# A four-layer graph network on one core: LayerNorm statistics two tiles at a time, a diagonal product moved to VectorE, two bias products moved to GpSimd, and a new order of the work

## The reference

```
L0: e = x@a_i [i] + x@a_j [j], normalised by its mean and variance over all pairs,
    e = e*adj + adj, leaky, softmax over i, h = sigmoid(alpha @ x)
L1: h = x@Wp + bp; masked GAT attention; h_gat = relu(layernorm(attn*A @ h))
    h_gin = (1+eps)*h_gat + A @ h_gat; z = relu(layernorm(h_gin@W1 + b1))
    out = relu(z@W2 + b2 + h_gat)
L2: A = softmax of the edge weights; out = diag(A) part @ (x@W0)
    + off-diagonal part @ (x@W1) + bias
L3: h = x@W; masked attention; elu(attn @ h)
```

## Time and profile before

| | before |
|---|---|
| median of three executions | 1191.42 us |
| span of the profiled execution, first to last instruction | 1188.6 us |
| PE / DVE / ACT / POOL busy | 93% / 89% / 81% / 50% |
| busy in 300 to 500 us of the span: PE / DVE / ACT / POOL | 195.76 / 189.68 / 175.35 / 110.70 of 200 us |
| granted TensorE clock in the loop | 1.00 (0.80 in the first 50 us) |

### The profile page before, as it was taken

How to read it: one execution, slowest core, us unless ns; L and a number is a source line. 1 busy time by engine, 2 the same in 40 slices (tenths; PEclk the granted TensorE clock), 3 DMA queues, 4 the chain that set the end, 5 groups by cost and what they waited for, 6 DMA issues and landing times.

```text
span 1188.6 us, 28920 instructions
## 1 busy us (share of the span) xinstructions
PE 1103.5 (93%) x7752; PEld 907.9 (76%) x7752; DVE 1055.8 (89%) x3894; ACT 964.7 (81%) x2453; POOL 594.6 (50%) x1250
## 2 busy tenths in 40 slices
PE   4779999999999999999999999999999999999964
PEld 3457777888777888887778888877778888788743
DVE  6887999999999999999999999999999899997642
ACT  3566888888888888888888889888888898888753
POOL 4243435555564555556555555555545554553422
PEclk7799999999999999999999999999999999999976
DMA  3010001110011111000111110101111010010000
GB/s 76 19 36 19 27 28 46 31 31 22 22 35 35 35 35 35 26 28 17 35 35 35 35 35 26 35 9 35 35 35 35 29 37 30 17 46 10 28 9 19
DMA packets 59478, 36.17 MB, mean 30 GB/s; under 512 B 3872, under 2 KB 54816, under 8 KB 59424
## 3 DMA queue, kind: packets, MB, share of 16 engines
q1 hardware_dynamic: 59424, 35.54, 10.0%
HBM read 18.75 MB, written 8.39 MB: 23 GB/s over the span
## 4 chain that ended last, share of the span: by engine, by line
PE 58%; POOL 10%; issue 9%; DVE 5%; ACT 2%; DMA 1%; POOLq 0%; SPq 0%; ACTq 0%; DVEq 0%
PE ps L965 14%; PE ps L893 7%; PE ps L949 6%; PE ps L982 4%; PE ps L1025 4%; PE ps L934 4%; PE ps L744 4%; PE ps L737 3%; POOL rirA L559 2%; PE ps L1014 2%; PE ps L880 2%; PE ps L1043 2%; PE ps L1042 2%; PE ps L919 1%; DMA xA<-in_x_dram 1%
## 5 line engine op out<-in xcount | busy, mean ns | idle before, releaser
L965 PE MATMUL ps<-hE,pTE 128*128 128x128 f32 x1024 | 131.0, 277 | 0.2
L982 PE MATMUL ps<-gin_j,hgat 128*128 128x512 f32 x256 | 124.4, 610 | 3.0 <-DVE gin_j L1495 1.8
L965 PE MATMUL ps<-hB,pTB 128*128 128x128 f32 x1024 | 125.3, 275 | 0.7 <-DVE pTB L1626 0.6
L893 PE MATMUL ps<-xsA,pA 128*128 128x128 f32 x1024 | 124.4, 275 | 0.0
L965 PEld LDWEIGHTS ps<-hE,pTE 128*128 128x128 f32 x1024 | 122.8, 193 | 0.9 <-issue 0.6
L1025 PE MATMUL ps<-att_j,xD 128*128 128x512 f32 x256 | 122.3, 601 | 0.8 <-ACT xD L2207 0.8
L965 PEld LDWEIGHTS ps<-hB,pTB 128*128 128x128 f32 x1024 | 119.4, 192 | 1.4 <-DVE pTB L1626 1.1
L893 PEld LDWEIGHTS ps<-xsA,pA 128*128 128x128 f32 x1024 | 119.4, 192 | 0.4 <-issue 0.3
L2250 ACT ACTIVATE pA<-vA,nmA,rirA 128x512 f32<-128x512 f32 x128 | 107.0, 845 | 6.3 <-DVE vA L1683 5.3
L2312 ACT ACTIVATE pE<-wE,mnE 128x512 f32<-128x512 f32 x128 | 92.4, 723 | 20.9 <-DVE mnE L1613 20.8
L1595 DVE SCALAR_TENSOR_TENSOR wE<-ps,hE,y2E 128x512 f32<-128x512 f32 x128 | 92.1, 739 | 13.8 <-ACT y2E L2282 13.7
(11 more groups left out here) (238 smaller groups left out, 3084.6 us busy)
## 6 DMA issues: line engine op xcount, KB each, us to landing
xA<-in_x_dram SPq DMA_DIRECT2D x32, 256.0 KB, 2.9
xrA<-in_x_dram SPq DMA_DIRECT2D x32, 256.0 KB, 2.7
xrB<-xB SPq DMA_DIRECT2D x32, 256.0 KB, 2.3
out_dram<-xout SPq DMA_DIRECT2D x32, 256.0 KB, 2.3
adj_i<-in_adj_dram SPq DMA_DIRECT2D x1, 1024.0 KB, 5.5
a<-in_L_gnn_a_dram SPq DMA_DIRECT2D x2, 64.0 KB, 5.1
w_sb<-in_L_gnn_W_dram SPq DMA_DIRECT2D x2, 64.0 KB, 3.7
l2w<-in_L_gnn_W_dram SPq DMA_DIRECT2D x2, 64.0 KB, 3.2
```

The lines of the kernel that those rows point to most:

```text
L893: last = mm(at("aggA")[:, i * P:(i + 1) * P], pA[:, j, i * P:(i + 1) * P], xsA[:, j], start=(j == 0), stop=(j == NT - 1))
L965: last = mm(at("agg" + n)[:, i * P:(i + 1) * P], att[n]["pT"][:, i, j], att[n]["h"][:, j, 0:P], start=(j == 0), stop=(j == NT - 1))
L982: last = mm(at("gin"), hgat[:, j], gin_j[:, j], start=(j == 0), stop=(j == NT - 1))
```

## The change

- **LayerNorm statistics.** bn_stats gets two tiles in one instruction, read as interleaved: element 0 of the first tile, element 0 of the second, element 1 of the first, and so on, 256 elements, with 512 bytes between neighbours in the order of reading. The instruction keeps statistics of even and odd elements apart, so its six results are the count, mean and squared deviation of either tile. Twelve bn_stats per graph take the place of 24, all 24 bn_aggr go, and `L["mean"]` and `L["m2"]` point into the results. rstd_k takes m2/128 + eps with one tensor_scalar on POOL, after the negative mean instead of ahead of it; for B it is a small DVE instruction, ve_B.
- **Diagonal part.** In the preparation the diagonal is spread over all partitions (spread_dia, copy_dia, a (128 x 512) tile diaT). Per graph, PE transposes xD (four transposes instead of four float32 products), and DVE multiplies the PSUM result with diaT into xTdD (diag_D). ACT's copy_xTD goes.
- **Two biases.** The bias products in x2_C and out_D go from PE. POOL adds b2 to hgat (bias_C, result hgb) and the layer-2 bias to xD (bias_D, result xDb), each one tensor_tensor of 128 x 512 with the bias row repeated; q_C and y_D read these. The split of the biases in the preparation covers 258 columns instead of 514.
- **Orders and banks.** All lists for PE, DVE, ACT and POOL are new, fill and drain included, and so is IN_BANK. SP's turn is as it was. The loop still has 22 turns.

```diff
+        def two_tiles(src, half):
+            return src[:, half * 2 * P:(half + 1) * 2 * P].rearrange("p (u d) -> p d u", u=2)
...
-                    pool.tensor_tensor(L["ve"][:], L["mv"][:, :, 1], eps, ALU.add).then_inc(s["ve_" + k], 1)
-                    pool.wait_ge(s["ve_" + k], g.now)
                     pool.wait_ge(s["applied0_B" if k == "B" else "applied_" + k], g.last)
-                    pool.tensor_tensor(L["nm"][:], L["mv"][:, :, 0], consts[:, 3:4].to_broadcast([P, NT]),
+                    pool.tensor_tensor(L["nm"][:], L["mean"], consts[:, 3:4].to_broadcast([P, NT]),
                                        ALU.mult).then_inc(s["nm_" + k], 1)
+                    if k != "B":
+                        pool.tensor_scalar(L["ve"][:], L["m2"], 1.0 / P, LN_EPS, ALU.mult, ALU.add).then_inc(s["ve_" + k], 1)
+                        pool.wait_ge(s["ve_" + k], g.now)
...
+            def bias_C(g):
+                pool.wait_ge(s["applied_B"], g.now)
+                pool.wait_ge(s["qC_ready"], g.last)
+                pool.tensor_tensor(hgb[:], hgat[:], bias_2, ALU.add).then_inc(s["hgb_ready"], 1)
+            def bias_D(g):
+                pool.wait_ge(s["applied_C"], g.now)
+                pool.wait_ge(s["y_D"], g.last)
+                pool.tensor_tensor(xDb[:], xD[:], bias_l2, ALU.add).then_inc(s["xDb_ready"], 1)
...
-                features("x2", zT, w2_sb[:], bias_2).then_inc(s["x2C_in_psum"], 1)
+                features("x2", zT, w2_sb[:]).then_inc(s["x2C_in_psum"], 1)
...
-                    last = mm(at("xTD")[:, i * P:(i + 1) * P], xD[:, i], dia[:, i], start=True, stop=True)
-                last.then_inc(s["xD_scaled"], 1)
+                transpose("xTD", xD).then_inc(s["xD_transposed"], 1)
...
-                mm(tiles(at("outD")), onesb[:], bias_l2, start=True, stop=False, skip_group_check=True)
...
-                    for i in range(NT):
-                        last = v.bn_stats(L["st"][:, i], y(i))
+                    for half in range(NT // 2):
+                        last = v.bn_stats(ln[k]["st"][:, half], two_tiles(src, half))
...
-                    for i in range(NT):
-                        last = v.bn_aggr(L["mv"][:, i], L["st"][:, i])
-                    last.then_inc(s["stats_" + k], 1)
...
+            def ve_B(g):
+                v.scalar_tensor_tensor(L["ve"][:], L["m2"], 1.0 / P, zzB[:], ALU.mult, ALU.add).then_inc(s["ve_B"], 1)
...
+            def diag_D(g):
+                dve.wait_ge(s["xD_transposed"], g.now)
+                dve.wait_ge(s["outD_ready"], g.last)
+                v.tensor_tensor(xTdD[:], at("xTD"), diaT, ALU.mult).then_inc(s["xTdD_ready"], 1)
...
-            def copy_xTD(g):
-                a.copy(xTdD[:], at("xTD")).then_inc(s["xTdD_ready"], 1)
...
-            [("tE", 5), ("z", 3)],
+            [("pB2", 3), ("h012E", 5), ("pE0", 5)],
```

More of the change, by code:

```diff
@@ new lines, in fill @@
+                t.once(triangles, numbers)
+                t.graph(0, variance_A, power_A, shift_A, high_A, rest_A0, middle_A)
+                t.once(loops_E)
+                t.graph(0, rest_A1, low_A)
+                t.graph(1, centre_A, square_A)
+                t.graph(0, rstd_A)
+                t.graph(1, variance_A, power_A, shift_A, high_A, rest_A0, middle_A, rest_A1, low_A)
+                t.graph(0, rstd_B)
+                t.graph(2, centre_A, square_A, variance_A, power_A, shift_A)
@@ L580, in fill @@
                 t.graph(1, rstd_A)
-                t.graph(0, rstd_Z)
-                t.once(loops_E, no_edge_E)
-                t.graph(0, rstd_C)
+                t.graph(2, high_A, rest_A0, middle_A, rest_A1, low_A)
+                t.graph(0, bias_C, rstd_Z, rstd_C)
                 t.graph(1, rstd_B)
-                t.graph(3, centre_A, square_A, variance_A, power_A, shift_A, high_A, rest_A0,
-                        middle_A, rest_A1, low_A)
+                t.graph(3, centre_A, square_A)
@@ L587, in fill @@
+                t.graph(0, bias_D)
+                t.graph(3, variance_A, power_A, shift_A)
                 t.graph(2, rstd_A)
+                t.graph(3, high_A, rest_A0, middle_A, rest_A1, low_A)
                 t.graph(1, rstd_Z)
+                t.once(no_edge_E)
+                t.graph(1, bias_C)
                 t.graph(0, rstd_D)
                 t.graph(1, rstd_C)
+                t.graph(4, centre_A, square_A)
                 t.graph(2, rstd_B)
-                t.graph(4, centre_A, square_A, variance_A, power_A, shift_A, high_A, rest_A0,
-                        middle_A, rest_A1, low_A)
+                t.graph(4, variance_A, power_A, shift_A)
@@ L594, in fill @@
                 t.graph(3, rstd_A)
-                t.graph(2, rstd_Z)
+                t.graph(4, high_A, rest_A0, middle_A, rest_A1, low_A)
+                t.graph(1, bias_D)
+                t.graph(2, bias_C, rstd_Z)
                 t.graph(1, rstd_D)
@@ L1704, in bn_B @@
                 dve.wait_ge(s["nm_B"], g.last)
-                for i in range(NT):
-                    last = v.bn_stats(ln["B"]["st"][:, i], at("aggB")[:, i * P:(i + 1) * P])
+                for half in range(NT // 2):
+                    last = v.bn_stats(ln["B"]["st"][:, half], two_tiles(at("aggB"), half))
                 last.then_inc(s["bn_B"], 1)
@@ L1832, in fill @@
+                t.graph(0, bn_C)
+                t.graph(1, bn_B, ve_B)
+                t.graph(3, dots_A0, dots_A1, mean_A)
+                t.graph(2, y_A)
+                t.graph(3, sumsq_A)
+                t.graph(2, bn_A)
                 t.graph(1, gain_B, offset_B)
-                t.graph(2, y_A, bn_A, join_A)
-                t.graph(3, v_A0, v_A1, lrelu_A0, lrelu_A1)
+                t.graph(0, diag_D)
+                t.graph(3, v_A0, v_A1, v_A2, v_A3, max_A, lrelu_A0, offset_A, lrelu_A1, lrelu_A2)
```

1436 lines of the change are left out of this document (688 added, 748 removed), and 9 rows, old and new, of the table IN_BANK.

## The result

The changed kernel takes 1233.71 us (1231.67 to 1235.83, 4 runs) against 1191.79 beside it; the ratio is 1.036, 95% interval [1.034, 1.038]. The forecast was 1168. The profiled run took 1235.83.

The account below looks back on a forecast made before the run. It took PE, the DVE/DMA path and POOL's vector chain as balanced, PE's turn falling from 33.75 to 33.0 us. 27 turns give -20.3, the ends -3: 1165.3 span, plus 2.8, 1168 us; range 1150 to 1194.

Parts of the forecast that it names:

- ACT's path: In the loop, last read of xA 26.5 us behind sum_A, plus 4.62 and 1.86: next sum_A at 33.0, as PE.
- the sum: PE's loop turn: 33.75 - 0.89 + 0.29 - 0.15 = 33.0 us, multiplied by 27 turns.
- The ends: Fill and drain together: -3 us, between 0 and -8; the new fill order was left unpriced.
- PE's work: Per turn on PE: bias products gone, -0.44 us, transposes for scale_xD's float32 products, -0.45; together -0.89.
- POOL's chain: rstd_A joins POOL's vector chain: wait ahead of rows_A on PE grows 0.29 us per turn, bounds -0.3 to +0.9.
- DVE: DVE's loop path: about 32.6 us per turn, just below PE's 33.0, so not bounding, 0.4 to spare.
- rival 1: POOL's long bias sums hold DVE 0.3 to 0.6 us each, or x2_C waits: turn 33.5 to 33.8, about 1186; chance 0.2.
- Rival 2: DVE's interleaved bn_stats read runs at half rate, 0.6 us instead of 0.33: turn 34.9, about 1220 us; chance 0.15.
- Rival 3: POOL's chain runs free of DVE, stall ahead of rows_A goes: turn 32.3, about 1148 us; chance 0.08.

Follow-up runs that it names:

- e1: Changed kernel with the next graph's xA load ahead of keep_xB and store in SyncE's queue; 1182.33 us, ratio 0.991 to the kernel before.
- e4: e1 with both bias products back on PE, POOL's two 128 x 512 sums gone; 1172.87 us, ratio 0.983 to the kernel before.
- e14: Changed kernel with only the fill mended: POOL's masks ahead of the first centring, weights' transposes and copies late; 1227.96 us, ratio 1.028 to the kernel before.
- e15: e4 with the fill mended as in e14, and rstd_A moved behind low_A on POOL; 1192.26 us.
- e7: e1 with bias_D and rstd_Z exchanged in POOL's turn, both sums on POOL; 1184.11 us, ratio 0.993 to the kernel before.
- e2: Changed kernel with the xA load between keep_xB and store in SyncE's queue; 1199.53 us, ratio 1.005 to the kernel before.

## Why the prediction was wrong, point by point

**The step that failed is ACT's path**, "with 4.62 and 1.86 the next sum_A is at 33.0". The working up to it held: the last read of xA was foretold 26.5 behind sum_A and started 26.69 behind it (595.79 - 569.10). But 4.62, from that read to dots_A, was carried over as a constant. It holds a place in SyncE's queue: the load stands behind keep_xB, and keep_xB behind y_C. In the changed kernel the 4.62 measures 602.07 - 595.79 = 6.28, and 26.69 + 6.28 + 1.84 = 34.81 is the undisturbed interval. The prediction priced what moved on DVE and never asked what else waits for the moved y_C. e1 puts the load ahead of keep_xB and gets 33.08 with nothing else changed. That this meets the sum's 33.0 is in part luck. In e1's turns of 32.80 the read starts at 26.47, as foretold, but from it to dots_A are 4.15 and from there to sum_A 2.18, and DVE's holds, which the forecast didn't price, are in every turn; e4, with the same queue, turns in 32.46, below the 33.0 that ACT's path was to allow. Of the 35.8 us that the loop lost, 21 x (34.85 - 33.75) = 23 are the wait, 10.5 the half clock, for which the sum had no term, and 1.9 the other three long intervals.

**The ends**, -3 foretold. As the sum multiplied by 27, six more intervals at -0.75 belong to them: -7.5 in all, and -15.8 for the 21 of the loop. Measured are +9.7 and +35.8. The drain gave 3.9. The fill took 13.6, of a kind that the prediction left unpriced: it said that the order of the fill "isn't to be had from the trace". The new order was at hand, and so was each wait: the counts behind a transfer that lands at 19 us, the masks behind DVE's first mean. In e14 the 7th sum_A is at 206.12, 7.8 earlier, and the median 5.75 to 7.9 less, as said above. The remaining 5.8 against 200.35 arise ahead of the second sum_A, 43.40 in e14 against 37.62, where DVE's list has more once-only work in front of the second graph's dots_A (it starts at 41.12 in e14, at 35.79 before). That this work is the cause was not tried.

**PE's work**, -0.89: the pieces measured as priced, but moving the bias products didn't pay. Taken off PE they save it 0.44, and the turn is 0.62 longer all the same, e1's 33.08 against e4's 32.46.

**POOL's chain**, +0.29: wrong in sign, at its own lower bound. The wait ahead of rows_A, 0.34 before, was to grow to 0.63. In e4 it is at most 0.28: rows_A comes 7.40 behind sum_A in the turns of 32.32 us and 7.68 in those of 32.60, and from squares_A to rows_A are 5.85 (514.63 - 508.78) instead of the foretold 6.95. rstd_A took 2.22, as priced, but the power took 0.69 where it had taken 1.16, and the split 1.71 where it had taken 2.07. In the new order it also has to stand there: in e15, with rstd_A behind the split, the turn is 1.2 us longer, since ACT's xB then comes late for its transposes. The price of one end of a chain was taken without what waits at the other.

**DVE**, 32.6: in the turn shown it would have reached the next sum_A at 600.02 + 1.84 - 569.10 = 32.76. The number is met, but 0.72 of it is a hold by hgb that the sum didn't have (rival 1); in e4, without holds, dots_A starts 30.14 behind sum_A without idle, which gives 31.98.

**Rival 1** was real and half mispriced: the sums take 1.09 where 1.2 was taken, each hold is up to 0.92 us long rather than 0.3 to 0.6, and where it falls depends on the order. In the changed kernel hgb meets M_E3 (POOL, DVE):

```profile
578.76 1.09 POOL L576 TENSOR_TENSOR hgb<-hgat,biases 128x512 f32<-128x512 f32 x1
```

```profile
579.00 1.40 DVE L1644 CUSTOM_DVE_ANT_0 wE<-wE,no_i 128x512 f32<-128x512 f32 x1
```

1.40 in place of 0.68. It isn't hidden by the idle in front of dots_A: no row of DVE from there to y_C in that turn shows an idle, so it delays y_C, for which the load waits. By how much the turn would be shorter without it is open, as no run has the late load without the sums. e1 and e4 show its price with the load early. The Trainium skill (SBUF — State Buffer, "Who interferes with whom") has the shared port as an exclusive lock, and these rows agree: lmA, the later starter, ends at 524.62 and xDb at 524.61; wE ends 0.55 behind hgb, less than the 0.68 that it takes alone.

**Rival 2** is false. All statistics of the changed kernel, by line (busy us, mean ns), one row of six; the earlier trace rows are those of before:

```profile
L1611 DVE BATCH_NORM_STATS2 lnst_C<-y_C 128x6 f32<-128x256 f32 x64 | 24.2, 421 | 0.0
```

0.42 us for 256 columns (0.28 for 128 before), pairs in 0.76, from SBUF and PSUM alike; from the start of a pair to the next operation are 598.56 - 597.89 = 0.67, where 0.66 was foretold. By the Trainium skill (Advanced Engine Details and Errata, "Memory Cachelines") reads that each fall in another line pay a penalty; for bn_stats, 512 bytes apart, none is seen. No run has a contiguous one of 256.

**Rival 3** named 32.3 for the turn without waits: e4 reaches 32.46, by another way than the one it gave.

## What to carry to other kernels

A time between two events of a trace is a constant only if everything on the way is: write down what stands ahead of a transfer in its queue, and for whom each of these waits, before carrying the distance over. When a change reorders an engine, look for unrelated work queued behind each moved result, on every queue, the one whose list isn't in the change first of all. If two waits end within a microsecond or two of each other, an experiment on one can show nothing; try both together.

## What the runs showed of the hardware that was not expected

In the changed kernel PE stood idle for 1.5 to 1.9 us ahead of all but the first of the loop's 21 sum_A, and behind eight of these idles its granted clock went to half for some 3.4 us, 10.5 us in all, 0.5 per turn. In e2, with idles of at most 0.7 there, and in e1, there were none between 300 and 900 us. Why it was these eight is open.

A POOL sum of 128x512 float32 takes 1.09 us (1.55 in e7, where an operation of DVE stood ahead of it) and makes an operation of DVE on SBUF wait up to 0.92 us, even one of four columns; DVE's operations with an input in PSUM ran beside it at their usual 0.69.
